# An MoE layer with linear attention: dispatched rows without the residual, which goes straight to the output and is added to by an accumulating scatter

## The reference

```python
xn  = layernorm(x)
a   = attn(xn)      # layer norm, q, k, v, gate; k = k * gate; q, k = elu + 1; causal linear attention, num / den
g   = sinkhorn gates of 8 experts per token; the best two are kept and scaled to sum 1
ffn = xn + sum over the two experts e of gate_e * ((relu(xn @ wg[e]) * (xn @ wp[e])) @ wo[e])
out = x + a + ffn
```

## Time and profile before

| | |
|---|---|
| Median of three runs | 364.75 us |
| Span of the profiled execution | 365.3 us |
| That span against the median | +0.55 us (0.15%) |
| PE busy | 331.2 us (91%) |
| POOL busy | 268.1 us (73%) |
| DVE busy | 268.4 us (73%) |
| ACT busy | 236.1 us (65%) |
| Moved by DMA | 70.97 MB, mean 194 GB/s |

### The profile page before, as it was taken

How to read it: one execution, slowest core, us unless ns; L and a number is a source line. 1 busy time by engine, 2 the same in 40 slices (tenths; PEclk the granted TensorE clock), 3 DMA queues, 4 the chain that set the end, 5 groups by cost and what they waited for, 6 DMA issues and landing times.

```text
span 365.3 us, 8755 instructions
## 1 busy us (share of the span) xinstructions
PE 331.2 (91%) x2560; PEld 301.9 (83%) x2560; DVE 268.4 (73%) x726; ACT 236.1 (65%) x437; POOL 268.1 (73%) x364
## 2 busy tenths in 40 slices
PE   0788989879999999998999999999999999999980
PEld 0678748647888888876999999999899999999970
DVE  3898889998988888887576676567666667667640
ACT  2669854323767667566777775788677777777530
POOL 3496999975777776557577777777777777777773
PEclk9999999987999999999999999999999999999995
DMA  6999999999344342348599987617665565572110
GB/s 172 255 295 336 333 334 307 290 297 275 121 145 146 105 145 89 117 115 249 164 318 377 346 246 203 173 54 194 187 196 158 151 172 164 150 225 74 50 39 5
DMA packets 64189, 70.97 MB, mean 194 GB/s; under 512 B 6002, under 2 KB 59006, under 8 KB 64144
## 3 DMA queue, kind: packets, MB, share of 16 engines
q1 hardware_dynamic: 54016, 48.70, 49.0%
q0 software_dynamic: 8672, 21.19, 16.0%
q10 hardware_dynamic: 1456, 0.53, 0.7%
HBM read 28.54 MB, written 43.04 MB: 196 GB/s over the span
## 4 chain that ended last, share of the span: by engine, by line
PE 75%; DVE 12%; DMA 3%; issue 3%; POOL 2%; SPq 2%; ACT 2%; POOLq 0%; ACTq 0%; DVEq 0%
PE psum L1765 17%; PE psum L1750 8%; PE psum L1752 8%; PE psum L1751 8%; PE psum L1572 4%; PE psum L1654 4%; PE psum L1636 4%; DMA rows<-in_L_attn_x 3%; PE psum L1463 3%; PE psum L1516 2%; POOL out L614 2%; PE psum L1740 2%; PE psum L1554 2%; PE psum L1557 2%; PE psum L1519 2%
## 5 line engine op out<-in xcount | busy, mean ns | idle before, releaser
L592 POOL DMA_INDIRECT by_lower<-rows,slot_u x64 | 64.4, 1006 | 28.7 <-issue 18.4
L614 POOL DMA_INDIRECT out<-rows x70 | 68.9, 985 | 21.4 <-issue 16.5
L1750 PE MATMUL psum<-xT_high,w_now 128*128 128x256 f32 x256 | 77.1, 301 | 1.9 <-DVE xT_low L1387 1.1
L1765 PE MATMUL psum<-w_expert,hT 128*128 x560 | 75.4, 276 | 1.0 <-DVE hT L1396 0.7
L825 ACT ACTIVATE w_now<-w_split 128x1024 fp32r x63 | 66.7, 1059 | 14.7 <-PE psum L1752 14.7
L1751 PE MATMUL psum<-xT_low,w_now 128*128 128x256 f32 x256 | 71.6, 280 | 0.0
L1752 PE MATMUL psum<-xT_high,w_now 128*128 128x256 f32 x256 | 71.5, 279 | 0.0
L603 POOL DMA_INDIRECT by_upper<-rows x58 | 57.2, 987 | 17.7 <-issue 11.6
L1400 DVE TENSOR_TENSOR hT<-relu,psum 128x512 f32<-128x512 f32 x64 | 44.0, 688 | 35.5 <-ACT relu L844 18.0
L1765 PEld LDWEIGHTS psum<-w_expert,hT 128*128 128x128 f32 x560 | 68.7, 191 | 1.4 <-issue 1.3
L844 ACT ACTIVATE relu<-psum 128x512 f32<-128x512 f32 x64 | 38.2, 598 | 22.0 <-PE psum L1752 21.9
(11 more groups left out here) (277 smaller groups left out, 660.3 us busy)
## 6 DMA issues: line engine op xcount, KB each, us to landing
by_lower<-blank SPq DMA_DIRECT2D x1, 10140.0 KB, 34.4
by_upper<-blank SPq DMA_DIRECT2D x1, 10062.0 KB
rows<-by_upper SPq DMA_DIRECT2D x32, 258.0 KB, 3.0
rows<-by_lower SPq DMA_DIRECT2D x26, 260.0 KB, 4.3
rows<-in_L_attn_x SPq DMA_DIRECT2D x8, 512.0 KB, 9.8
lead_row<-by_lower SPq DMA_DIRECT2D x6, 260.0 KB
out<-rows POOLq DMA_INDIRECT x70, 2.5
w_expert<-in_L_ffn_wg SPq DMA_DIRECT2D x8, 128.0 KB, 2.5
```

The costliest lines, as they stand in the source:

```text
L592: pool.indirect_dma_start(by_lower, bass.IndirectOffsetOnAxis(ap=slot_u[:, t:t + 1], axis=0), rows[:, t, :], None)\
L614: pool.indirect_dma_start(out_rows, bass.IndirectOffsetOnAxis(ap=row(n)[:, k, TOKEN:TOKEN + 1].bitcast(U32), axis=0), row(n)[:, k, BASE], ...
L1750: pe.matmul(target, high, x_high, start=True, stop=False)
L1765: last = pe.matmul(psum[:, 4 + n % 2, k * D:(k + 1) * D], hT[:, n % 3, f, k * P:(k + 1) * P], weights, start=(f == 0), stop=(f == FB - 1))
```

## The change

Base plus attention no longer travels with the rows. The rows in `by_lower` have 132 columns instead of 260 (z, gates, token, slot), the clear of `by_lower` and the loads from it shrink accordingly, and its scatters wait for the slots alone, no longer for `row_done`. SP stores base plus attention of each group straight to `out` (`store_out`, 16 plain DMAs of 256 KB). The first pass's `save_y` writes gate times y without adding anything; the second pass's adds its own as before, and its scatters add to `out` in the DMA (`compute_op=ALU.add`) after all 16 stores have landed. The semaphore `scattered` is split in three.

```diff
+    Y = BASE
+    SENT, KEPT = slice(D, ROW), slice(0, ROW_UP)
...
-    by_lower = nc.dram_tensor("by_lower", ((NBLOCK + 1) * W, ROW), F32).ap()
+    out_view = out.rearrange("b (c p) d -> b p c d", p=P)
+    by_lower = nc.dram_tensor("by_lower", ((NBLOCK + 1) * W, ROW - D), F32).ap()
...
+        RING_GROUPS = -(-2 * NB // G)
...
             sp.dma_start(by_lower.rearrange("(n p) r -> p n r", p=P),
-                         blank[:].unsqueeze(1).to_broadcast([P, 2 * (NBLOCK + 1), ROW])).then_inc(lower_cleared, 16)
+                         blank[:, SENT].unsqueeze(1).to_broadcast([P, 2 * (NBLOCK + 1), ROW - D])).then_inc(lower_cleared, 16)
...
+            def store_out(n):
+                sp.wait_ge(row_done, (n + 1) * G)
+                b, c0 = n // GB, G * (n % GB)
+                sp.dma_start(out_view[b][:, c0:c0 + G, :], rows[:, n * G:(n + 1) * G, BASE])\
+                    .then_inc(ring_stored if n < RING_GROUPS else rest_stored, 16)
...
                 if n == 0:
                     sp.wait_ge(q_ready, NG - 1)
+                    sp.wait_ge(scattered_soon, 16 * SOON)
                 if n < LEAD:
-                    sp.wait_ge(scattered, sp.value_load(lead_need[:, n:n + 1], min_val=16 * SOON, max_val=16 * NT))
+                    sp.wait_ge(lead_open, sp.value_load(lead_need[:, n:n + 1], min_val=1, max_val=2))
                 if n == LEAD:
-                    sp.wait_ge(scattered, 16 * NT)
+                    sp.wait_ge(scattered_late, 16 * (NT - SOON))
+                    sp.wait_ge(ring_stored, 16 * RING_GROUPS)
...
-                sp.dma_start(row(n)[:, 0:tiles, 0:columns],
+                sp.dma_start(row(n)[:, 0:tiles, columns],
...
-            for e in range(1, E - 1):
-                sp.wait_ge(o_ready, FREED_BY[e] + 1)
-                load_expert(e)
+            for n in range(NG - 2):
+                for e in range(1, E - 1):
+                    if FREED_BY[e] == n:
+                        sp.wait_ge(o_ready, n + 1)
+                        load_expert(e)
+                store_out(n)
             sp.wait_ge(route_dve, TABLES_STEP)
             for n in range(LEAD):
-                load_row(n, by_lower, ROW)
+                load_row(n, by_lower, SENT)
             for n in range(LEAD, NE):
+                if n == LEAD + 2:
+                    store_out(NG - 2)
+                    store_out(NG - 1)
...
-                load_row(n, by_lower, ROW)
+                load_row(n, by_lower, SENT)
             for n in range(NE, 2 * NE):
-                load_row(n, by_upper, ROW_UP)
+                load_row(n, by_upper, KEPT)
...
+            pool.sem_inc(lead_open, 1)
             pool.wait_ge(lower_cleared, 16)
             pool.wait_ge(route_dve, SLOTS_STEP)
-            for n in range(NG):
-                for t in range(n * G, (n + 1) * G):
-                    if t == SOON:
-                        pool.wait_ge(scattered, 16 * SOON)
-                    pool.wait_ge(row_done, t + 1)
-                    pool.indirect_dma_start(by_lower, bass.IndirectOffsetOnAxis(ap=slot_u[:, t:t + 1], axis=0),
-                                            rows[:, t, :], None)\
-                        .then_inc(scattered, 16)
+            for t in range(NT):
+                pool.indirect_dma_start(by_lower, bass.IndirectOffsetOnAxis(ap=slot_u[:, t:t + 1], axis=0),
+                                        rows[:, t, SENT], None)\
+                    .then_inc(scattered_soon if t < SOON else scattered_late, 16)
+
+            pool.wait_ge(scattered_late, 16 * (NT - SOON))
+            pool.sem_inc(lead_open, 1)
...
+            pool.wait_ge(ring_stored, 16 * RING_GROUPS)
+            pool.wait_ge(rest_stored, 16 * (NG - RING_GROUPS))
             for n in range(NE, 2 * NE):
...
                     pool.indirect_dma_start(out_rows, bass.IndirectOffsetOnAxis(
                         ap=row(n)[:, k, TOKEN:TOKEN + 1].bitcast(U32), axis=0),
-                        row(n)[:, k, BASE], None, bounds_check=last_token, oob_is_err=False)\
+                        row(n)[:, k, Y], None, bounds_check=last_token, oob_is_err=False, compute_op=ALU.add)\
                         .then_inc(row_out[q], 16)
...
-                link(dve.tensor_scalar(lead_need[:], lead_late[:], 16.0 * (NT - SOON), 16.0 * SOON, ALU.mult, ALU.add))
+                link(dve.tensor_scalar(lead_need[:], lead_late[:], 1.0, None, ALU.add))
...
                 for k in range(width(n)):
-                    target = row(n)[:, k, BASE]
-                    dve.scalar_tensor_tensor(target, psum[:, 4 + n % 2, k * D:(k + 1) * D],
-                                             row(n)[:, k, by:by + 1], target, ALU.mult, ALU.add)\
-                       .then_inc(y_saved, 1)
+                    target, y = row(n)[:, k, Y], psum[:, 4 + n % 2, k * D:(k + 1) * D]
+                    if n < NE:
+                        dve.tensor_scalar(target, y, row(n)[:, k, GATE_LOW:GATE_LOW + 1], None, ALU.mult).then_inc(y_saved, 1)
+                    else:
+                        dve.scalar_tensor_tensor(target, y, row(n)[:, k, GATE_UP:GATE_UP + 1], target, ALU.mult, ALU.add)\
+                           .then_inc(y_saved, 1)
```

More of the change, by code:

```diff
@@ L267, in sparse_block_kernel @@
         x_in = [sem(f"x_in{b}") for b in range(B)]
-        (v_loaded, w_loaded, const_ready, lower_cleared, upper_cleared, scattered) = steps(
-            "v_loaded w_loaded const_ready lower_cleared upper_cleared scattered")
+        (v_loaded, w_loaded, const_ready, lower_cleared, upper_cleared, scattered_soon, scattered_late, lead_open) = steps(
+            "v_loaded w_loaded const_ready lower_cleared upper_cleared scattered_soon scattered_late lead_open")
+        (ring_stored, rest_stored) = steps("ring_stored rest_stored")
         (rw_loaded, rw_pe, rw_step, w_scaled, w_summed, w_sum_saved, w_step) = steps(
@@ L1404, in save_y @@
                 dve.wait_ge(wo_done, n + 1)
-                by = (GATE_LOW, GATE_UP)[n // NE]
                 for k in range(width(n)):
-                    target = row(n)[:, k, BASE]
-                    dve.scalar_tensor_tensor(target, psum[:, 4 + n % 2, k * D:(k + 1) * D],
-                                             row(n)[:, k, by:by + 1], target, ALU.mult, ALU.add)\
-                       .then_inc(y_saved, 1)
+                    target, y = row(n)[:, k, Y], psum[:, 4 + n % 2, k * D:(k + 1) * D]
[4 more added lines that the diff above has]
+                           .then_inc(y_saved, 1)
             for a in range(2):
```

## The result

The changed kernel takes 406.44 us (median of 4 runs, 404.91 to 406.82), the kernel before 364.85 us on the same chip (364.55 to 367.27). The ratio is 1.111, 95% interval 1.107 to 1.114: slower by 11%, where 367.4 us was forecast. The profiled execution of the changed kernel has a span of 405.1 us (before: 365.3), so 39.8 us are to be found.

What follows compares the result with a forecast made beforehand. POOL's back-to-back scatters through both passes were taken to set the end. 365.3 - 0.07 + 1.5 + 1.2 = 367.9 us, less 0.55 from profiled span to median: 367.4 us, range 364.0 to 387.

Steps and rivals of the forecast that it cites:

- first y of pass 1, then 70 scatters, then 70 scatters, then the landing: The chain taken to set the kernel's end: POOL back to back through both passes, 1.291 us a scatter step.
- The edits priced at nothing: Slot-only waits of `by_lower` scatters, half the clear and loads, 16 stores on SP's queue: each forecast at 0 at the end.
- second-pass scatters add: POOL's 70 second-pass scatters to `out`, adding in the DMA: 0.022 us each, +1.5 us; bounds 0 to 69 us.
- a median above 1.1 us for the adding scatter: Stated sign of a wrong forecast, on POOL's second pass: the sum would then be 70 times the excess.
- B: Rival: a real price on POOL, 0.1 to 0.3 us per adding scatter, 373 to 387 us in all; 20%.
- C: Rival: on POOL the add's read side doubles and is all of the cost, 70 x 0.985 us, so 435 us; 13%.
- the nearest row for one thing more per row: The bounds check on POOL's scatters, 22 ns for 128 rows, taken as the price of each add.
- The low end: Lower bound for the add on POOL: nothing, since POOL's time does not follow the bytes.
- `save_y` without its add: First-pass `save_y` on VectorE: 346 ns becomes about 280 ns, only the first on the path, -0.07 us.
- The last landing: After the last scatter to `out`: an add also reads the rows it writes, +1.2 us; bounds 0 and 3.0 us.
- E: Rival: faster, the first y comes earlier and shortens POOL's idle before 179.51 by at most 2.4 us, 362.3 us; 6%.

Runs made afterwards that it cites:

- the plain version of the change: The changed kernel with its second-pass scatter writing instead of adding, so base plus attention is overwritten; 365.25 us over 12 runs, 1.0007 of the kernel before.

## Why the prediction was wrong

The mechanism was the right one, and one size in it was wrong.

**What held.** The chain "first y of pass 1, then 70 scatters, then 70 scatters, then the landing" describes the changed kernel as it did the one before, and the other runs with 128 rows; with fewer rows POOL waits for many of the y. One joint is not POOL's alone: at the seam of the changed kernel the first y of the second pass came last, and POOL idled 1.00 us there. The edits priced at nothing were worth nothing that can be measured: the plain version of the change is at 1.0007 of the kernel before. By their own signs: the `by_lower` scatters were to end near 170.4 with gaps of 0.30 and ended at 170.2 with 63 of 64 gaps POOL's own; the first lead load was forecast for 164.7 and went at 163.6; PE turned its entry at 171.68 with no wait for a row in front of it. SP's queue and PE in the changed kernel, which answer to the earlier trace rows:

```profile
161.31 0.39 SPq L421 DMA_DIRECT2D out<-rows  x1
163.61 9.38 SPq L447 DMA_DIRECT2D lead_row<-by_lower  x6
```

```profile
171.68 0.60 PE L1675 MATMUL psum<-ident,lead_row 128*128 128x128 f32 x4
173.40 0.36 PE L1771 MATMUL psum<-xT_high,w_now 128*128 128x256 f32 x1 [1.13 <-DVE xT_low L1407]
```

**The step that failed** is "second-pass scatters add": 70 x 0.022 = +1.5 us. Measured: 70 x 0.573 = +40.1. The prediction's own sign of being wrong came true, "a median above 1.1 us for the adding scatter (then B or C, and the sum is 70 times the excess)". The place was right (on the chain that ends last, 70 times, nothing beside it), and so were the bounds, 0 to 69 us. What was wrong is the choice between them. The prediction went to "the nearest row for one thing more per row", the bounds check; but that row prices a check on a plain scatter, and nothing tied the price of an add to it. The runs show the add to be another price: about 0.4 us for each adding instruction, at 32 rows as at 128, and 1.2 ns more for each row. The check has no such fixed part: scatters with it (L621) take 27, 9 and -2 ns more than those without (L608) at 128, 64 and 32 rows (985 and 958, 902 and 893, 867 and 869). The low end was also leaned on for a reason that doesn't carry: that POOL's time doesn't follow the bytes was true before and stayed true for the adding scatter (1560 ns at half the bytes), and its price was still there.

**The rivals.** B had the cause at 0.1 to 0.3 us, and C at 0.985; the truth, 0.57, lay in the gap between them, with 20% on one side and 13% on the other. C expected the read side to double all of the cost. The rows do nearly double in price (1.3 to 2.5 ns each), but that is only a quarter of the loss. The Trainium skill states two source reads per add ("Collectives: The Full Stack", The bandwidth ceiling); the price per row would fit that, but the packets also go from 16 to one per row, and no run tells the two apart. Against the Trainium skill's remark that descriptor generation is small ("DMA: Bandwidth & Descriptors", Anatomy of one DMA — SWDGE (gpsimd) path) the measurement decides: at 70 instructions back to back, generation is what sets the end.

**The range** stopped at 387 because C was the case left out. With a bound of 69 us on the ending chain and no row of the operation, the middle of that bound should have been inside it.

**The small terms.** `save_y` without its add was put at -0.07 us; its median is 344 ns on the lead rows and 346 on the others, against the 346 of the earlier trace rows, so 0: the form with one tensor source takes as long as the form with two. The last landing was put at +1.2 us: the median landing rose by 0.8 (2.5 to 3.3), but the span ends 5.0 us after the last scatter where it was 5.4, so nothing of it shows at the end. E's earlier first y (177.78 instead of 178.37) is within what this start differs by from run to run.

**What stays open:** what POOL does in the 0.4 us that follow neither rows nor bytes, and why a plain scatter behind an adding one costs 0.05 us more. The traces show one record per instruction and nothing inside it.

## What to carry to other kernels

One operand, which makes a plain scatter an adding one, took its price on POOL from 0.985 to 1.56 us here. Price such an operand as unknown until a trace has a row of it, and where it stands on the chain that ends last, multiply the whole of its bound by its count before choosing a value inside. Before work is moved onto such a chain to relieve something else, ask whether what is relieved is on it: here the waits, the clear and the loads that the change saved were all under cover. A scatter that must add would belong where POOL has slack (not tried here). Its price was not cut by half the bytes or by rows out of bounds, and a quarter of the rows cut it only from 1.56 to 1.31 us.

## What the runs showed of the hardware that was not expected

- An adding indirect scatter of 128 rows costs POOL 1.56 us against 0.985, of which about 0.4 us are there at 32 rows too. It sends 112 packets more (by the counts 128 where a plain one sends 16), and POOL's queue keeps the DMA engines busy for 0.36 of 340 to 350 us against 0.14.
- A plain scatter that follows an adding one costs 0.05 us more (1.03 against 0.983, 35 scatters of one run).
- A row that the check drops costs POOL as much as a row that is sent (1560 ns at half the tokens) and leaves its packet behind.
- The plain scatter has a large fixed part too: 0.867 us at 32 rows, 0.985 at 128.
